# Edge lists loaded as 96 partitions and the rest, features loaded as 120 and 5 partitions at the end of the preparation's DMA list

## The reference

```
x: [12500, 128] f32     src, dst: [200000] i32, sorted by dst     edge_attr_128: [200000, 128] f32
h = relu(layernorm(x)); x = x + sage3(h)      # 3 rounds: relu([h, mean of h[src] by dst] @ W + b)
h = relu(layernorm(x)); x = x + gat(h)        # attention over edges and self loops, then an MLP
h = relu(layernorm(x)); x = x + gin(h)        # sum of relu(h[src] + edge_attr), MLP with batch norm
h = relu(layernorm(x)); x = x + (h + sum of (h[src] + edge_attr) by dst)
```

## Time and profile before

| | us |
|---|---|
| median of 3 runs | 13256.12 |
| lowest and highest of the 3 | 13250.01, 13263.81 |
| the profiled execution | 13269.17 |
| its span | 13267.2 |
| POOL busy in it | 9013.3 (68%) |
| PE busy in it | 6021.2 (45%) |
| DVE busy in it | 3452.2 (26%) |
| preparation, to the first DVE instruction of stage 2 | 191.92 |

### The profile page before, as it was taken

How to read it: one execution, slowest core, us unless ns; L and a number is a source line. 1 busy time by engine, 2 the same in 40 slices (tenths; PEclk the granted TensorE clock), 3 DMA queues, 4 the chain that set the end, 5 groups by cost and what they waited for, 6 DMA issues and landing times. The chain is left out here.

```text
span 13267.2 us, 102459 instructions
## 1 busy us (share of the span) xinstructions
PE 6021.2 (45%) x27058; PEld 4761.4 (36%) x27059; DVE 3452.2 (26%) x6432; ACT 1221.1 (9%) x2429; POOL 9013.3 (68%) x9490
## 2 busy tenths in 40 slices
PE   3444444344444444444354444665444546333333
PEld 2433333333333333333344333433333333333333
DVE  4222222111111222222344444452222225111111
ACT  1000000000000000000011000042222222000000
POOL 1777776777777677777577777217777760777776
PEclk9555555555555555555566666587666678555555
DMA  3222222222222222222333333223333332222222
GB/s 101 55 55 55 55 55 51 54 55 55 55 56 55 59 67 67 67 68 70 72 86 86 84 84 84 67 98 102 105 102 102 102 95 103 61 61 61 61 61 58
DMA packets 519276, 956.93 MB, mean 72 GB/s; under 512 B 173853, under 2 KB 328106, under 8 KB 517588
## 3 DMA queue, kind: packets, MB, share of 16 engines
q0 software_dynamic: 301056, 623.59, 18.6%
q1 hardware_dynamic: 218112, 332.26, 8.1%
HBM read 847.12 MB, written 108.07 MB: 72 GB/s over the span
## 5 line engine op out<-in xcount | busy, mean ns | idle before, releaser
L744 POOL DMA_INDIRECT work<-rows_a,index x4704 | 4468.3, 950 | 1595.7 <-issue 1550.6
L772 PE MATMUL psum<-onehot,work 128*128 128x80 f32 x12544 | 2713.2, 413 | 4079.1 <-DMA work<-rows_a,index 2948.1
L772 PEld LDWEIGHTS psum<-onehot,work 128*128 128x128 f32 x12544 | 2628.4, 322 | 4166.4 <-issue 4165.5
L1496 POOL DMA_INDIRECT regionC<-attention_rows,index x1568 | 1526.6, 974 | 548.3 <-issue 477.6
L913 POOL DMA_INDIRECT work<-rows_b,index x1568 | 1491.6, 951 | 567.4 <-issue 518.7
L744 POOL DMA_INDIRECT work<-rows_b,index x1568 | 1480.7, 944 | 540.6 <-issue 518.1
L996 PE MATMUL psum<-regionB,onehot 128*80 128x256 f32 x3136 | 939.1, 473 | 1022.3 <-ACT regionB L973 1022.3
L831 DVE TENSOR_TENSOR regionA<-regionA,psum 128x80 f32 x784 | 185.3, 236 | 4523.3 <-PE psum L772 4314.0
L996 PEld LDWEIGHTS psum<-regionB,onehot 128*80 128x80 f32 x3136 | 589.1, 192 | 1344.6 <-issue 1222.0
L184 POOL COPY work<-regionB 128x500 f32 (+1 forms) x75 | 45.3, 603 | 977.7 <-DVE regionB L653 977.7
L1060 DVE TENSOR_TENSOR regionB<-work,psum 128x512 f32<-128x512 f32 x392 | 243.1, 682 | 1528.8 <-DMA work<-rows_b,index 1528.8
(11 more groups left out here) (347 smaller groups left out, 6956.3 us busy)
## 6 DMA issues: line engine op xcount, KB each, us to landing
regionB<-in_edge_attr SPq DMA_DIRECT2D x195, 512.0 KB
work<-rows_a,index POOLq DMA_INDIRECT x4704, 2.5
work<-rows_b,index POOLq DMA_INDIRECT x3136, 2.5
work<-edge_columns SPq DMA_DIRECT2D x98, 512.0 KB
regionC<-attention_rows,index POOLq DMA_INDIRECT x1568
x_transposed<-regionA SPq DMA_DIRECT2D x75, 250.0 KB, 6.3
rows_a<-regionC SPq DMA_DIRECT2D x50, 250.0 KB
regionB<-h_transposed SPq DMA_DIRECT2D x2, 5250.0 KB, 17.0
```

The lines of the kernel that those rows point to most:

```text
L744: pool.indirect_dma_start(rows3[h][:, t, :], None, table, bass.IndirectOffsetOnAxis(ap=net.index[:, k, h * ST + t:h * ST + t + 1], axis=0) ...
L772: last = nc.tensor.matmul(bank_of(h, q, 0), rows3[h][:, t, :], onehot[:, h * ST + t, :], start=(k == 0), stop=(k == GT - 1))
L1496: pool.indirect_dma_start(ring[s][:, t, :], None, net.XH, bass.IndirectOffsetOnAxis(ap=net.index[:, k, t:t + 1], axis=0)).then_inc(gathere ...
```

## The change

The full partitions of `dst` and `src` are loaded by two DMAs in place of one, 96 partitions and then the 97th; the rest of 1,344 numbers follows as before. So each list has three loads, and the waits for them count to 48. The features are loaded by two DMAs in place of five, partitions 0 to 119 and 120 to 124, each with all 100 row groups, and these stand between the edge columns and the wait for the 96 copies. The last wait counts two of them.

```diff
             for name, to, sem in (("dst", dst_i, loaded_d), ("src", src_i, loaded_s)):
-                sp.dma_start(to[0:whole, :], net.dram[name][0:whole * GPH * GE]
-                             .rearrange("(p f) -> p f", p=whole)).then_inc(sem, 16)
+                even = whole // 16 * 16
+                sp.dma_start(to[0:even, :], net.dram[name][0:even * GPH * GE]
+                             .rearrange("(p f) -> p f", p=even)).then_inc(sem, 16)
+                sp.dma_start(to[even:whole, :], net.dram[name][even * GPH * GE:whole * GPH * GE]
+                             .rearrange("(p f) -> p f", p=whole - even)).then_inc(sem, 16)
                 sp.dma_start(to[whole:whole + 1, 0:left], net.dram[name][whole * GPH * GE:E]
                              .rearrange("(p f) -> p f", p=1)).then_inc(sem, 16)
-            for k in range(5):
-                sp.dma_start(net.C[0:SUB, k * 20 * D:(k + 1) * 20 * D].rearrange("p (t f) -> p t f", f=D),
-                             net.dram["x"][k * 2500:(k + 1) * 2500, :]
-                             .rearrange("(t p) f -> p t f", p=SUB)).then_inc(features, 16)
             sp.wait_ge(step, 4)
...
             for a in range(2):
                 sp.dma_start(net.RELROW[:, a, :].rearrange("p (q e) -> p q e", e=TILE),
                              rel4_f.rearrange("p (q a e) -> p a q e", a=2, e=TILE)[:, a]).then_inc(wrote, 16)
+            for lo, hi in ((0, 120), (120, SUB)):
+                sp.dma_start(net.C[lo:hi, 0:NSUB * D].rearrange("p (t f) -> p t f", f=D),
+                             net.dram["x"].rearrange("(t p) f -> p t f", p=SUB)[lo:hi]).then_inc(features, 16)
             sp.wait_ge(copied, len(tiles))
...
-            sp.wait_ge(features, 80)
+            sp.wait_ge(features, 32)
...
-            dve.wait_ge(loaded_d, 32)
+            dve.wait_ge(loaded_d, 48)
...
-            dve.wait_ge(loaded_s, 32)
+            dve.wait_ge(loaded_s, 48)
```

## The result

| | before | after |
|---|---|---|
| median of 6 runs each, us | 13259.97 | 13203.57 |
| lowest and highest, us | 13250.01, 13279.44 | 13192.68, 13207.40 |
| ratio of the times | | 0.9953, 95% interval 0.9943 to 0.9963 |
| span of the profiled execution, us | 13267.2 | 13190.8 |
| preparation, to the first DVE instruction of stage 2, us | 191.92 | 124.92 |

The change makes the kernel faster by 0.47%, 56 us (the interval is 49 to 76). The forecast was 13165.6 with a range of 13150 to 13192: right in direction, its gain of 90.5 us 1.6 times the measured one, and the measured time is outside the range. In the profiled executions the preparation is 67.0 us shorter, where the prediction had 90.5. The spans differ by 76.4; I put the 9.4 us beyond the preparation down to scatter between executions: the profile of before was of a run above its median and that of after of the fastest one.

What follows compares the result with a forecast made beforehand. POOL's edge gathers set the pace, unchanged; the preparation counts one for one. L496 100.4 us earlier, less 10.7 us of features sticking out, put stage 2 90.5 us earlier: 13256.12 becomes 13165.6 us, range 13150 to 13192.

Steps and rivals of the forecast that it cites:

- What bounds the kernel: Whole kernel: POOL's edge gathers set the pace; stages do not overlap, so changes to the 192 us preparation count one for one.
- Edge lists: Preparation, loads of `dst` and `src`: split lists land sooner, L443 starting near 10.0 (27.6 us earlier), L484 40.5 us earlier.
- Features off SP's front: Preparation, write of `dst_padded` no longer held behind feature loads: the 60.00 us wait goes, L496 at 33.8, 100.4 us earlier.
- Features at the end: End of preparation: feature loads take 22.5 us, 10.7 beyond the copies; stage 2 starts at 101.4, 90.5 us earlier.
- B: Rival, feature load: lists speed up, but 120 partitions get 8 engines (13181 us) or 5 (13203 us), not 15; chance 0.08.
- A: Rival, preparation loads: splitting by partitions spreads neither lists nor features; stage 2 only 12.8 us earlier, 13243 us; chance 0.04.
- C: Rival, PE's clock: the grant falls inside stage 2 and two later dense stretches, 244 us more, 13410 us; chance 0.03.
- D: Rival, feature load: the 120-partition load falls to one engine, 277 us more than taken, 13442 us; chance 0.01.

## Why the prediction was wrong

**What bounds the kernel: right.** The time of the preparation goes into the total one for one, within a scatter of about 10 us: over the nine pairs of medians the gain in the total lies between 11 us below and 12 us above the gain in the stage.

**Edge lists: right, 1.6 us short.** L445 at 11.61, where 10.0 was forecast and the bounds were 9 to 13. The lists no longer went on one engine: from 7 to 12 us the DMA share is 0.88 to 1.12, but at 213 to 319 GB/s rather than 420. The wait for `src` vanished.

**Features off SP's front: right.** L498 at 35.49 for 33.8, 98.7 us earlier for 100.4. The write of `dst_padded` was issued when DVE was ready for it. The flag writes drained at about 70.

**Features at the end: this step failed.** The prediction took each of 15 engines at the rate that each of 5 had, 21.4 GB/s, 22.5 us in all, with the flags' 263 GB/s as the other end, and let them stick out by 10.7 us. Measured: 167 to 187 GB/s, some 37 us for the 120 partitions, which end at about 106 for 91.4; and from there to stage 2 it took 18.9 us for the 10.0 taken for tables and landing, since the five partitions, at one engine's rate, held back their engines with the tables behind. Stage 2 starts at 124.9 for 101.4: 14.6 and 8.9 us are the 23.5 by which the sum was wrong. The number of engines was about as I had read it from the rows of before (a share of 1.13). What did not carry over was the rate of one of them. A rate per engine is not a property of the engine alone: the rows from which I bounded it, 25 partitions for each of 5 engines and 7 for each of 14, gave 21.4 and 18.8 GB/s for each engine, and 8 for each of 15 gave 11 to 12. Both ends lay on the same side of the truth; twice the lower one, 43 us, would have been near it. The other 10.6 us between the forecast gain of 90.5 and the median's 56.4 are the scatter spoken of above: the 67.0 us of the stage lie inside the measured 49 to 76.

**Rivals.** B gave 13203 for a load that gets only 5 engines, and the measured time is 13203.57, but it is not B: the engines were 15, and five engines, in the old form at the new place, were 16 us slower. The totals meet by luck: of the 38.0 us between forecast and measured time 23.5 are the stage's, 3.9 come from the median of before, which is higher with six runs than with three, and 10.6 are the scatter. A, the rule that two transfers to disjoint partitions serialise, is out for the lists: they landed 26 us earlier. For the features the gain of the split is 16 us where three times the engines should have given 37, but not because two transfers serialised: in the run with the five partitions early the 120 go without their neighbours and still at 148 to 193 GB/s. The sentence that A drew on, in the Trainium skill's "DMA: Bandwidth & Descriptors", section "Rules for kernel authors", gives as its reason that both transfers share the same engines; it does not say that each keeps its old rate, so A read more into it than it has. The same section's rule of the Trainium skill, to issue early and wait late, decides little here: from SP, early and late differ by 2 us at most; from ACT, which holds up nobody, early gains 5.6. My reading that the early load was to blame was half right: the lists alone, with the feature loads still early, gain 52.7 of the 67.0, since the features no longer queue behind some 60 us of lists on one engine. C and D did not come: the granted clock is 1.00 in the first 50 us of stage 2's dense part and 0.86 in the next 44 (0.87 before), 1.00 in the later stretches of 120 and 60 us, and no feature row below 100 GB/s but for the five partitions.

## What to carry to other kernels

Count for a DMA not only the engines it will use but how its partitions are dealt to them: here blocks of 8 partitions for each of 15 engines had about half the rate for each engine, and a remainder of five partitions moved at the rate of one engine while the tables waited behind it. Where a tensor has 125 partitions and space for 128, load 128 and let three be junk (the last row group, which has nothing behind it to read, goes by itself). If an engine has nothing to do, let it issue the load. And where a transfer is to be split in a new way, let half the rate seen be one end of its price, unless a row of the trace has the same split.

## What the runs showed of the hardware

The rates of reads in pieces of 512 bytes by the way they were split, all from this case: 125 partitions (5 engines, 25 each) 109 GB/s; 120 (15 engines, 8 each) 167 to 187 in the first profile, 148 to 193 over all six runs that have it; 112 (16 engines, 7 each) 219 to 258; 128 (16 engines) 290 to 296; partitions 120 to 124 (5 engines, one each) 20 to 24. The numbers of engines are read from the shares, and that each has an equal block is assumed.

The Trainium skill has the map that fits them, in "SBUF — State Buffer", section "Door 1: The DMA port swizzle (why `[64,N]` ≈ `[32,N]`)": SBUF takes DMA writes through 16 ports, four neighbouring partitions share one, and so do partitions 32 apart within a half. I did not draw on it in the prediction. If engine e of 15 works through partitions 8e to 8e+7 in step with the others, as I assume (no trace here says which engine writes where), then by that map only 8 of the 16 ports are written at any time, and two engines share each but one: half the rate, an estimate of 8 times 21.4 or 171 GB/s by the rate of one engine in this trace, with 148 to 193 measured. This takes it that a port has no more than one engine's 21.4 GB/s to give, which no run tests, and it does not say why the same load varies from run to run. Of partitions 120 to 124 four lie behind one port: one engine's rate, 21.4, with 20 to 24 measured. For 112 partitions the same map and assumptions have the slowest engine take nine partitions' time for its seven, an estimate of 7/9 of 342 or 266 GB/s, a little above what came. That ports and partitions pair in this way is what the page of the Trainium skill says, and the rates agree with it; the runs themselves show only that the rate follows the partitions and neither the addresses in HBM nor the number of rows. Why 128 partitions reach 290 and not 16 times 21.4, 342, stays open.
